# Projecting q and k from a copy of x by columns, with the tokens' mean and scale as rows

## The chip, the cores and the metric

One core of a Trainium2 chip runs the whole kernel. The metric is the device time of one execution in microseconds (us), the median of the runs.

## The reference

```python
x = x + attn(layernorm(x), q_proj, k_proj, v_proj, o_proj)   # x: (1, 2048, 256), 16 heads of 16, causal softmax
x = x + ffn(layernorm(x), W, b, lora_A, lora_B, gate_w, gate_b)
# layernorm: (x - mean) / sqrt(var + 1e-5), over the 256 features
# attn: q, k, v = ln @ W.T; scores / 4; masked softmax; @ v; @ o_proj.T
# ffn: ln @ W.T + b, plus the LoRA updates (8 experts of rank 16) of the two
#      experts with the largest logits, weighted by a softmax over those two
```

All inputs and the output are f32.

## The kernel before

The 2048 tokens are 16 tiles of 128, four tiles a chunk (TPC = 4, CHUNK = 512, NCHUNK = 4). P is 128, KH is 2: the 256 features are two halves of 128 partitions. Every normalised tile is turned on TensorE, because the projections contract over features and so need x with features on partitions, tokens on columns.

The first chunk is projected ahead of everything (`project_first_chunk` on each engine). Then the attention runs in 138 steps. Step s computes two units of scores, 2s and 2s+1 (`scores_of`, L682: f16, two banks a unit, q and k each split in a high and a low f16 part and stacked on 64 rows), takes their exponentials on ScalarE (L814), clears later keys on VectorE one step later (`clear_later_keys`, L999; only units on the diagonal), and multiplies by v into `acc` some steps later (`values_of`, L702, f32). Chunk 0 has steps 0 to 9, chunk 1 steps 10 to 35, chunk 2 steps 36 to 77, chunk 3 steps 78 to 135. On TensorE a step is: the scores of two units, the piece of slot 0, the values of the groups of that step, the piece of slot 1 (only chunk 0 has pieces in slot 1).

Everything else is cut into pieces that share one PSUM bank, `aux`; a piece waits until the piece before it has been read from that bank (`bank_read`, L419). `place_pieces` (L124) gives each piece its step at build time, in order, one a slot. Pieces that prepare the next chunk come first, three for a tile: `turn_x` (L585: two transposes of the normalised tile `xln` by the identity), `project_qk` (L591: 4 blocks x 2 halves, 128 columns each, into all of `aux`), `project_v` (L600). Then `norm_q` and `norm_k`, sums of squares which decide at the end whether the fast softmax was allowed. Then come the pieces after attention, seven for a tile: `turn_sums`, `turn_back`, `o`, `turn_y`, `ffn`, `turn_gated`, `lora`, at most two tiles in work at a time. The four tiles of the last chunk come in a tail behind the steps.

For tile g, VectorE works beside these pieces: `measure_x` (L923: mean and variance), GpSimd the power of -1/2 (`rstd_x`, L1206), VectorE `normalise_x` (L934: `xln`), after the turn `store_xT` (L939), after ScalarE's copy `store_qk` (L801, the f32 result into `qk32`) `split_qk` (L945: high part, low part, clamp, square), and `store_v` (L963). Each engine's program is in a fixed order; VectorE's for a step is in `step` (listing below): normalise_y or the gates of the piece one step before, masks, the work of the piece in slot 0, `keep_sums`, the work of the piece in slot 1.

SyncE issues all DMAs, in a fixed order: the first loads (L431 to L438), q and k of the first chunk out to DRAM and back as stacks (L467 to L475, L450 to L465), the f32 q and k out (L522), `load_rest` (L440), then for each tile `store_parts` (L477: six DMAs), and after the last tile of a chunk 16 loads of stacks. The stack of queries has two buffers, `q_stack[:, c % 2]`; in the opening the second holds `first_parts`.

## Time and profile before

| | us |
|---|---|
| median of 3 runs | 394.41 (393.88 to 394.71) |
| the profiled execution, its own time | 393.18 |
| its span, first to last instruction | 391.4 |
| PE busy | 354.2 (90%) |
| ACT (ScalarE) busy | 279.5 (71%) |
| DVE (VectorE) busy | 209.7 (54%) |
| POOL (GpSimd) busy | 47.8 (12%) |
| mean granted TensorE clock | 0.975 |

The first scores are issued 21.7 us into the span; step 10 begins at 64.1 us; the last values end at 365.3 and the tail ends the span. Busy time of PE counts stretches in which matmuls are in its pipeline; PEld is the loading of weights, which overlaps it. 1.8 us of the profiled execution lie outside its span.

### The profile page before, as it was taken

How to read it: one execution, taken by the hardware profiler on the slowest of the kernel's cores; microseconds unless marked ns; L12 is line 12 of the kernel's file. 1: busy time of each engine (PE TensorE's matmuls, PEld its weight loads, DVE VectorE, ACT ScalarE, POOL GpSimd, SP SyncE). 2: the span in 40 equal slices, each digit the busy share in tenths (PEclk: the TensorE clock that was granted, in tenths of full speed). 3: DMA queues.
4: the chain of work that ended last, by engine and by line, in shares of the span. 5: the costliest groups of instructions: out<-in, count | busy, mean ns of one | idle time of the engine just before them, and what ended most of it. 6: DMA issues, size and time to landing. Idle time of an engine off the chain costs nothing.

```text
span 391.4 us, 6977 instructions
## 1 busy us (share of the span) xinstructions
PE 354.2 (90%) x2558; PEld 138.0 (35%) x2558; DVE 209.7 (54%) x711; ACT 279.5 (71%) x317; POOL 47.8 (12%) x75
## 2 busy tenths in 40 slices
PE   8967978899998999999999999998999899799874
PEld 3545524354333444423323233232322323222542
DVE  4555558455755654555447464546346543600785
ACT  2544438677887877888788887888878688799311
POOL 5011000000011100011121111211112111100040
PEclk9997969999999999999999999999999999999997
DMA  6479444222450022271000000000000000000001
GB/s 202 139 224 315 116 131 141 55 55 54 124 148 13 2 54 75 62 214 44 13 2 13 3 13 16 3 13 2 13 16 0 16 0 15 13 2 3 0 3 55
DMA packets 29380, 23.31 MB, mean 60 GB/s; under 512 B 15392, under 2 KB 25888, under 8 KB 29344
## 3 DMA queue, kind: packets, MB, share of 16 engines
q1 hardware_dynamic: 29344, 22.84, 19.8%
q8 instruction: 21, 0.34, 0.4%
q14 instruction: 15, 0.12, 0.1%
HBM read 12.35 MB, written 10.49 MB: 58 GB/s over the span
## 4 chain that ended last, share of the span: by engine, by line
PE 63%; DVE 20%; ACT 7%; issue 6%; POOL 2%; DMA 1%; DVEq 0%; ACTq 0%
PE acc L713 23%; PE scores L696 12%; PE aux L596 7%; ACT probs L814 6%; PE aux L651 5%; PE aux L637 3%; DVE probs L1010 2%; PE aux L662 2%; PE aux L602 2%; PE aux L623 1%; DVE ffn L1055 1%; POOL exp_gap L1216 1%; PE aux L644 1%; DVE gates L1083 1%; DVE parts L954 1%
## 5 line engine op out<-in xcount | busy, mean ns | idle before, releaser
L814 ACT ACTIVATE probs<-scores 128x1024 f32<-128x1024 f32 x272 | 260.2, 1032 | 69.1 <-PE scores L696 59.1
L713 PE MATMUL acc<-probs,v_aug 128*32 128x512 f32 (+3 forms) x1280 | 145.4, 545 | 1.3 <-ACT probs L814 0.9
L696 PE MATMUL scores<-q_stack,k_stack 64*128 64x512 f16 (+3 forms) x640 | 86.5, 352 | 3.7 <-ACT probs L814 2.0
L696 PEld LDWEIGHTS scores<-q_stack,k_stack 64*128 64x128 f16 x640 | 21.1, 94 | 103.6 <-ACT probs L814 80.3
L1010 DVE TENSOR_TENSOR probs<-probs,mask_sb 128x512 f32<-128x512 f32 (+1 forms) x80 | 44.2, 577 | 22.5 <-ACT probs L814 22.0
L713 PEld LDWEIGHTS acc<-probs,v_aug 128*32 128x32 f32 x1280 | 30.8, 110 | 49.8 <-issue 29.7
L596 PE MATMUL aux<-xT,wqkv_sb 128*128 128x128 f32 x192 | 26.3, 294 | 1.0 <-DVE xT L941 1.0
L596 PEld LDWEIGHTS aux<-xT,wqkv_sb 128*128 128x128 f32 x192 | 24.0, 203 | 5.4 <-issue 3.1
L952 DVE CAST parts<-qk 128x512 f16<-128x512 f32 x12 | 5.1, 427 | 36.5 <-ACT qk L806 36.5
L1207 POOL TENSOR_TENSOR rstd<-ve,minus_half 128x1 f32<-128x1 f32 x12 | 7.3, 608 | 101.6 <-DVE ve L932 101.6
L1211 POOL TENSOR_TENSOR rstd<-ve,minus_half 128x1 f32<-128x1 f32 x12 | 6.6, 549 | 103.8 <-DVE ve L1040 103.8
L651 PE MATMUL aux<-wffn_sb,yT 128*128 128x392 f32 x48 | 19.0, 518 | 0.0
L1033 DVE TENSOR_TENSOR y<-aux,x_sb 128x256 f32<-128x256 f32 x12 | 5.1, 424 | 23.9 <-PE aux L637 23.9
L1216 POOL TENSOR_TENSOR exp_gap<-euler,top_gap 128x1 f32<-128x1 f32 x12 | 6.6, 550 | 86.3 <-DVE top_gap L1068 86.3
L1055 DVE COPY ffn<-aux 128x392 f32<-128x392 f32 x12 | 6.8, 567 | 19.0 <-PE aux L651 19.0
L1015 DVE COPY sums<-acc 128x512 f32<-128x512 f32 x16 | 11.0, 686 | 7.0 <-PE acc L713 7.0
L602 PE MATMUL aux<-wqkv_sb,xT 128*128 128x256 f32 x48 | 13.6, 405 | 1.2 <-ACT qk L806 1.0
L1044 DVE TENSOR_SCALAR yln<-y,mv,rstd 128x256 f32<-128x256 f32 x12 | 9.7, 811 | 8.0 <-POOL rstd L1211 8.0
L637 PE MATMUL aux<-wo_sb,attn_t 128*128 128x256 f32 x48 | 13.6, 405 | 0.0
L1104 DVE TENSOR_TENSOR result<-aux,yb 128x256 f32<-128x256 f32 x12 | 5.1, 425 | 14.7 <-PE aux L662 14.7
L806 ACT COPY qk<-aux 128x512 f32<-128x512 f32 x12 | 7.0, 585 | 8.1 <-PE aux L596 5.6
L657 PE MATMUL aux<-ident_sb,gated 128*128 128x128 f32 x12 | 3.9, 327 | 9.0 <-DVE attn_t L1027 8.1
(146 smaller groups left out, 323.0 us busy)
## 6 DMA issues: line engine op xcount, KB each, us to landing
q_stack<-q_dram SPq DMA_DIRECT2D x32, 128.0 KB, 2.8
k_stack<-k_dram SPq DMA_DIRECT2D x32, 128.0 KB, 2.8
qk_dram<-qk SPq DMA_DIRECT2D x12, 256.0 KB, 2.5
x_sb<-x SPq DMA_DIRECT2D x3, 512.0 KB, 6.4
q_dram<-parts SPq DMA_DIRECT2D x12, 128.0 KB, 2.0
k_dram<-parts SPq DMA_DIRECT2D x48, 32.0 KB, 1.9
out<-result SPq DMA_DIRECT2D x12, 128.0 KB, 1.7
qk_dram<-probs SPq DMA_DIRECT2D x4, 256.0 KB, 3.3
```

The source lines that it names most:

```text
L596: m = pe.matmul(aux[:, n * P:(n + 1) * P], wqkv_sb[:, k, col:col + P], xT[:, k, :], start=(k == 0), stop=(k == KH - 1))
L602: m = pe.matmul(aux[:, 0:D], xT[:, k, :], wqkv_sb[:, k, 2 * D:3 * D], start=(k == 0), stop=(k == KH - 1))
L637: m = pe.matmul(w.bank[:, 0:D], w.attn_t[:, k, :], wo_sb[:, k, :], start=(k == 0), stop=(k == KH - 1))
L651: m = pe.matmul(w.bank[:, 0:FFN], w.yT[:, k, :], wffn_sb[:, k, :], start=(k == 0), stop=(k == KH - 1), skip_group_check=True)
L696: m = pe.matmul(scores[u % BANKS][:, j, col:col + n], k_stack[row:row + STACK, kb // TPC, 2 * i + p, kb % TPC * P:(kb % TPC + 1) * P], q_s ...
L713: m = pe.matmul(acc[32 * hp:32 * hp + 32, lo:CHUNK], v_aug[:, kb, QUAD * i + hp, :], probs[:, u % PROBS, hp % 2, col:col + CHUNK - lo], st ...
L814: act.activation(probs[:, u % PROBS], scores[u % BANKS][:], ACT.Exp, scale=EXP_SCALE).then_inc(exp_done, 1)
L1010: dve.tensor_tensor(tile, tile, mask, ALU.min).then_inc(causal_done, 1)
L1015: dve.tensor_copy(sums[:, c % 3, i, :], acc[:]).then_inc(acc_read, 1)
L1044: dve.tensor_scalar(w.yln, w.y, w.mv2[:, 0:1], w.rstd2, ALU.subtract, ALU.mult).then_inc(yln_ready, 1)
L1055: dve.tensor_copy(w.ffn, w.bank[:, 0:FFN]).then_inc(ffn_ready, 1)
L1216: pool.tensor_tensor(w.exp_gap, euler[:], w.top_gap, ALU.pow).then_inc(gap_exp, 1)
```

## The change

A second input holds x by columns: `x_t`, for each chunk 128 partitions (features) x 2 halves x 512 tokens, 512 KB a chunk, arranged on the host. A chunk is loaded into `xT` by one DMA of SyncE. `xln` and the pieces `turn_x` are gone. VectorE measures the four tiles of a chunk from `x_sb` as before (`measure_x(c, t)`), GpSimd raises all four variances at once, and then stores means and scales (`rows1`, 128 x 2 x 4 values) to DRAM in the order of the tokens, waits for that, waits until the buffer is free, and loads them back as two rows of 512 for every partition, into a part of `q_stack` that isn't in use yet. VectorE then subtracts the row of means from each half of `xT` and multiplies it by the row of scales (`normalise_x(c, k)`, two tensor_tensor of 128 x 512 a half).

`project_qk(n)` now computes one block, q or k of one half of the heads, for all 512 tokens: two matmuls of 512 columns. Four such pieces make a chunk, so their number is the same. `store_qk` and `split_qk` handle such a block; the clamped values go straight into `squares`. SyncE stores a block by one DMA (q) or two (k) and one for the f32 values, 10 a chunk where it was 24, and loads the stacks of a half as soon as its k has landed.

Placing: chunk 0 has its first piece in step 2, then q or k and v in turn, two a step, in steps 2 to 5, and the four norm pieces in steps 6 and 7. For chunk 2 the measurements are at steps 7 to 10, normalise_x at 15 and 16, the four project_qk at 17 to 20, the four project_v at 21 to 24, the norms at 25 and 26. For chunk 3: 33 to 36, 41 and 42, 43 to 46, 47 to 50, 51 and 52. The other pieces keep their order and take the steps left: turn_sums of tile 0 is at step 12 (before: 24), o at 14, turn_sums of tile 1 at 15, turn_y of tile 0 at 16, its ffn at 27; turn_gated of tile 2 is at 53; the last piece is at step 117 (before: 123).

```diff
@@ placing @@
-PRE_PIECES = ("turn_x", "project_qk", "project_v")
+FIRST = ((0, 0), (1, 0), (0, 1), (1, 1))
+FIRST_PIECE = 2
+MEASURE_FROM = {c: FIRST_STEP[c - 1] - 3 for c in range(2, NCHUNK)}
+NORMALISE_FROM = {c: MEASURE_FROM[c] + TPC + 4 for c in range(2, NCHUNK)}
...
-            for g in range(TPC * (c + 1), TPC * (c + 2)):
-                pre += [(name, g) for name in PRE_PIECES]
+            qk = [("project_qk", len(FIRST) * c + n) for n in range(len(FIRST))]
+            v = [("project_v", TPC * (c + 1) + t) for t in range(TPC)]
+            pre = [p for both in zip(qk, v) for p in both] if c == 0 else qk + v
...
-                if pre:
+                if pre and s >= (FIRST_PIECE if c == 0 else NORMALISE_FROM[c + 1] + 2):
@@ tiles @@
-        xln = sb("xln", [P, D])
-        xT = sb("xT", [P, KH, P])
+        rows1 = sb("rows1", [P, 2, TPC])
+        rows = [q_stack[:, b, 0:4].bitcast(F32).rearrange("p (n a) t -> p n (a t)", n=2) for b in range(2)]
+        xT = sb("xT", [P, KH, CHUNK])
@@ sync @@
             sp.dma_start(x_sb[:, TPC:2 * TPC, :], x[:, TPC:2 * TPC, :]).then_inc(x_in[1], 16)
+            sp.dma_start(xT[:], x_t[1]).then_inc(xT_in[1], 16)
+
+            def load_xT(c):
+                sp.wait_ge(v_psum, TPC * (c - 1))
+                sp.dma_start(xT[:], x_t[c]).then_inc(xT_in[c], 16)
...
+            def store_parts(n):
+                c, (kq, m) = n // len(FIRST) + 1, FIRST[n % len(FIRST)]
+                sp.wait_ge(low_ready, n + 1)
+                if kq == 0:
+                    sp.dma_start(q_dram[c, m].rearrange("s p t -> p s t"), parts[:, 0]).then_inc(parts_out[0], 16)
+                else:
                     for s in range(2):
-                        sp.dma_start(k_dram[c, m, :, s, :, tokens], parts[:, b, 1, m, s, :]).then_inc(parts_out[b], 16)
+                        sp.dma_start(k_dram[c, m, :, s], parts[:, 1, s, :]).then_inc(parts_out[1], 16)
+                sp.dma_start(qk32_dram[c, kq, m], qk32[:, kq]).then_inc(qk32_out[kq], 16)
@@ tensor @@
-            def turn_x(g):
-                pe.wait_ge(xln_ready, g - TPC + 1)
+            def project_qk(n):
+                c, (kq, b) = n // len(FIRST) + 1, FIRST[n % len(FIRST)]
+                pe.wait_ge(xT_ready, KH * c)
+                col = column_of(kq, b)
                 for k in range(KH):
-                    t = pe.transpose(aux[:, k * P:(k + 1) * P], xln[:, k * P:(k + 1) * P], ident_sb[:])
-                t.then_inc(xT_psum, 1)
+                    m = pe.matmul(aux[:], wqkv_sb[:, k, col:col + P], xT[:, k, :],
+                                  start=(k == 0), stop=(k == KH - 1))
                 m.then_inc(qk_psum, 1)
@@ vector @@
-                store_first_low(0)
-                store_first_low(1)
-                square_first(0)
-                square_first(1)
-                store_first_low(2)
-                store_first_low(3)
-                square_first(2)
-                square_first(3)
-                measure_x(TPC)
-                normalise_x(TPC)
-                store_xT(TPC)
+                for n in range(len(FIRST)):
+                    store_first_low(n)
+                    measure_x(1, n)
+                for n in range(len(FIRST)):
+                    square_first(n)
...
+            def normalise_x(c, k):
+                n = KH * (c - 1) + k + 1
+                dve.wait_ge(xT_in[c], 16)
+                dve.wait_ge(rows_in, 16 * c)
+                x_rows = xT[:, k, :]
+                dve.tensor_tensor(x_rows, x_rows, rows[c % 2][:, 0, :], ALU.subtract).then_inc(centred, 1)
+                dve.wait_ge(centred, n)
+                dve.tensor_tensor(x_rows, x_rows, rows[c % 2][:, 1, :], ALU.mult).then_inc(xT_ready, 1)
...
+                if s == FIRST_PIECE - 1:
+                    for k in range(KH):
+                        normalise_x(1, k)
+                for c in range(2, NCHUNK):
+                    if 0 <= s - MEASURE_FROM[c] < TPC:
+                        measure_x(c, s - MEASURE_FROM[c])
+                    if 0 <= s - NORMALISE_FROM[c] < KH:
+                        normalise_x(c, s - NORMALISE_FROM[c])
                 for u in (2 * s - 2, 2 * s - 1):
                     if 0 <= u < len(UNITS) and UNITS[u].masked:
                         clear_later_keys(u)
@@ gpsimd @@
-            def rstd_x(g):
-                pool.wait_ge(stats1, STATS1 * (g - TPC + 1))
-                pool.tensor_tensor(rstd1[:], ve1[:], minus_half[:, 0:1], ALU.pow).then_inc(rstd1_ready, 1)
+            def rstd_x(c):
+                pool.wait_ge(stats1, STATS1 * c)
+                if c > 1:
+                    pool.wait_ge(rows_out, 16 * (c - 1))
+                pool.tensor_tensor(rows1[:, 1, :], ve1[:].rearrange("p t o -> p (t o)"), minus_half[:],
+                                   ALU.pow).then_inc(rstd1_ready, 1)
+                pool.wait_ge(means_ready, c)
+                pool.wait_ge(rstd1_ready, c)
+                pool.dma_start(rows_dram[c].rearrange("n (t p) -> p n t", p=P), rows1[:],
+                               allow_slow_non_contiguous=True).then_inc(rows_out, 16)
+                pool.wait_ge(rows_out, 16 * c)
+                if c > 1:
+                    pool.wait_ge(scores_ready, FIRST_UNIT[c - 1])
+                else:
+                    pool.wait_ge(squared, len(FIRST))
+                    for m in range(KH):
+                        pool.wait_ge(first_q_out[m], 16)
+                        pool.wait_ge(first_k_out[m], 16 * 2)
+                pool.dma_start(rows[c % 2], rows_dram[c].partition_broadcast(P)).then_inc(rows_in, 16)
```

## Rows read from the trace of the kernel before

**Rows 1.** Page, parts 1 and 2: busy time; granted TensorE clock in 40 slices (tenths).
```profile
PE 354.2 (90%) x2558; PEld 138.0 (35%) x2558; DVE 209.7 (54%) x711; ACT 279.5 (71%) x317; POOL 47.8 (12%) x75
...
PEclk9997969999999999999999999999999999999997
```

**Rows 2.** Windows: stretch, length, busy of PE, PEld, DVE, ACT, POOL (x), clock, DMA.
```profile
35.50:43.40 7.90, 7.90 (x51) 5.13 (x50) 3.98 (x12) 2.52 (x3) 0.92 (x1) 0.66 0.77 224
...
52.80:64.00 11.20, 10.75 (x99) 4.05 (x98) 7.07 (x13) 6.41 (x7) 0.00 (x0) 0.77 0.68 201
```

**Rows 3.** Chain that ended last, in time: start us, us, engine, tile, line, count.
```profile
10.82 1.72 PE acc L572 x4
...
66.71 1.98 PE aux L596 x16
```

**Rows 4.** Groups by line and shape: total busy us, mean ns, idle before.
```profile
L1010 DVE TENSOR_TENSOR probs<-probs,mask_sb 128x512 f32<-128x512 f32 x48 | 31.9, 684 | 2.8 <-ACT probs L814 2.5
...
L954 DVE TENSOR_TENSOR parts<-qk,parts 128x512 f16<-128x512 f32 x12 | 8.3, 692 | 0.4
...
L588 PE MATMUL aux<-ident_sb,xln 128*128 128x128 f32 x24 | 5.5, 312 | 6.3 <-DVE v_aug L965 5.1 <-DVE xln L936 1.2
...
L806 ACT COPY qk<-aux 128x512 f32<-128x512 f32 x12 | 7.0, 585 | 8.1 <-PE aux L596 5.6 <-DMA qk_dram<-qk 2.5
```

**Rows 5.** DMA issues: queue, count, KB each, median us to landing.
```profile
x_sb<-x SPq DMA_DIRECT2D x3, 512.0 KB, 6.4
q_dram<-parts SPq DMA_DIRECT2D x12, 128.0 KB, 2.0
...
k_dram<-q_stack SPq DMA_DIRECT2D x4, 128.0 KB, 2.4
```

**Rows 6.** Timeline, opening: start us, us, engine line op (idle before, releaser).
```profile
18.21 0.42 DVE L921 TENSOR_TENSOR squares<-squares 128x512 bf16<-128x512 bf16 x1
...
19.55 1.22 SPq L475 DMA_DIRECT2D k_dram<-q_stack  x2
...
24.92 0.43 DVE L952 CAST parts<-qk 128x512 f16<-128x512 f32 x1 [2.70 <-ACT qk L806]
...
26.31 0.43 DVE L959 TENSOR_TENSOR squares<-clamped 128x512 bf16<-128x512 bf16 x1
...
30.49 0.22 PEld L696 LDWEIGHTS scores<-q_stack,k_stack 64*128 64x128 f16 x6
...
60.58 0.61 PE L696 MATMUL scores<-q_stack,k_stack 64*128 64x512 f16 x6
```

**Rows 7.** Timeline of PE: one turn_x piece that waits for VectorE.
```profile
74.54 0.44 PE L588 MATMUL aux<-ident_sb,xln 128*128 128x128 f32 x2 [1.42 <-DVE v_aug L965]
```

**Rows 8.** Timeline, 108 to 114 us: tile 0 after o, tile 1 turned.
```profile
108.81 0.42 DVE L1033 TENSOR_TENSOR y<-aux,x_sb 128x256 f32<-128x256 f32 x1 [1.56 <-PE aux L637]
...
110.83 0.81 DVE L1044 TENSOR_SCALAR yln<-y,mv,rstd 128x256 f32<-128x256 f32 x1 [0.73 <-POOL rstd L1211]
...
112.42 0.97 DVE L1010 TENSOR_TENSOR probs<-probs,mask_sb 128x256 f32<-128x256 f32 x2
...
113.22 0.44 PE L644 MATMUL aux<-ident_sb,yln 128*128 128x128 f32 x2
```

**Rows 9.** Timeline of PE: turn_gated after turn_back, without and with masks beside.
```profile
254.54 0.33 PE L657 MATMUL aux<-ident_sb,gated 128*128 128x128 f32 x1 [0.74 <-DVE attn_t L1027]
...
304.89 0.33 PE L657 MATMUL aux<-ident_sb,gated 128*128 128x128 f32 x1 [1.94 <-DVE attn_t L1027]
```

**Rows 10.** Timeline of PE: scores of four steps with no piece.
```profile
344.88 0.60 PE L696 MATMUL scores<-q_stack,k_stack 64*128 64x512 f16 x4
...
346.41 0.60 PE L696 MATMUL scores<-q_stack,k_stack 64*128 64x512 f16 x4
...
349.54 0.91 PE L696 MATMUL scores<-q_stack,k_stack 64*128 64x512 f16 x4
...
351.37 0.91 PE L696 MATMUL scores<-q_stack,k_stack 64*128 64x512 f16 x4
```

More of the change, by code:

```diff
@@ L317, in transformer_block @@
         stats1 = sem("stats1")
+        means_ready = sem("means_ready")
         rstd1_ready = sem("rstd1_ready")
-        xln_ready = sem("xln_ready")
-        xT_psum = sem("xT_psum")
+        rows_out = sem("rows_out")
+        rows_in = sem("rows_in")
+        xT_in = [sem(f"xT_in{c}") for c in range(NCHUNK)]
+        centred = sem("centred")
         xT_ready = sem("xT_ready")
@@ L663, in lora @@
                           skip_group_check=True).then_inc(out_psum, 1)
-            PRE = {"turn_x": turn_x, "project_qk": project_qk, "project_v": project_v, "norm_q": norm_q,
+            PRE = {"project_qk": project_qk, "project_v": project_v, "norm_q": norm_q,
                    "norm_k": norm_k, "turn_sums": turn_sums}
@@ new lines, in split_qk @@
+            def split_qk(n):
+                c, (kq, m) = n // len(FIRST) + 1, FIRST[n % len(FIRST)]
+                use = n // 2
+                high, low = (parts[:, kq, s, :] for s in range(2))
+                if use:
+                    dve.wait_ge(parts_out[kq], 16 * (kq + 1) * use)
+                dve.wait_ge(qk32_ready, n + 1)
+                dve.tensor_copy(high, qk32[:, kq]).then_inc(high_ready, 1)
+                dve.wait_ge(high_ready, n + 1)
+                dve.tensor_tensor(low, qk32[:, kq], high, ALU.subtract).then_inc(low_ready, 1)
+                block_of = squares[:, c % 2, KH * kq + m, :]
+                if c > 1:
+                    dve.wait_ge(norm_psum, 2 * (c - 2) + kq + 1)
+                dve.tensor_scalar(block_of, high, 1e15, -1e15, ALU.min, ALU.max).then_inc(clamped_ready, 1)
+                dve.wait_ge(clamped_ready, n + 1)
+                dve.tensor_tensor(block_of, block_of, block_of, ALU.mult).then_inc(squared, 1)
@@ L1104, in finish @@
                 dve.tensor_tensor(w.result, w.bank[:, 0:D], w.yb, ALU.add).then_inc(result_ready, 1)
-            PRE = {"turn_x": store_xT, "project_qk": split_qk, "project_v": store_v, "norm_q": norm_q,
+            PRE = {"project_qk": split_qk, "project_v": store_v, "norm_q": norm_q,
                    "norm_k": norm_k}
@@ L1226, in _ @@
                                    minus_half[:, 0:2], ALU.pow).then_inc(first_scale_ready, 1)
-            rstd_x(TPC)
-            rstd_x(TPC + 1)
-            for name, n in PIECES:
-                if name == "turn_x" and n + 1 < TILES:
-                    rstd_x(n + 1)
+            waiting = list(range(2, NCHUNK))
+            rstd_x(1)
+            for s, slot in sorted(PIECE_AT):
+                name, n = PIECE_AT[s, slot]
+                if waiting and s >= MEASURE_FROM[waiting[0]] + TPC:
+                    rstd_x(waiting.pop(0))
                 if name == "o":
```

142 lines of the change are left out of this document (56 added, 86 removed).

## The prediction

> **What bounds the kernel now.** I read the busy times first [rows 1]: PE is busy 354.2 of 391.4 us, so at most 37 us are waits of PE, and the other engines matter by when they release it. Then the windows [rows 2] for where PE is slow rather than idle: at 35.5 to 43.4 us it is busy all the time at a granted clock of 0.66, the first low stretch after it had waited, and 0.77 at 52.8 to 64. Then PE's timeline, step by step. A step with no piece and one group of values takes 1.53 us from scores to scores when PE sets the pace (344.88 to 346.41), and 1.83 us when ScalarE does, with its two exponentials (349.54 to 351.37) [rows 10]. Nearly every step before 123 has a piece, so there PE sets the pace and work taken from it counts in full; a step without a piece gives back only down to 1.83. Last, PE's waits for VectorE inside pieces: 1.42 us at a turn_x [rows 7], 0.74 us at a turn_gated behind the turn_back of the next tile, 1.94 us where two masks stand beside it [rows 9].
>
> **PE's work from chunk 1 on.** Of the 11 turn_x pieces that have a place, 8 lie in steps 10 to 47. The twelve with the one ahead of the steps keep PE busy 5.5 us [rows 4], 0.46 each with an overlap on both sides; I take 0.4, so 8 x 0.4 = 3.2 us. Projecting q and k costs 16 instructions of 128 columns a tile, 1.98 us; the first chunk does the same kind of work with 4 instructions of 512 columns in 1.72 us [rows 3]. Four tiles against four (q or k, half) blocks: 8 x 0.26 = 2.1 us for the two later chunks. project_v is as before. Together -5.3. The waits at turn_x go too: 1.42 [rows 7] and some tenths at another, -1.7.
>
> **What the free steps give back.** With 8 pieces fewer from step 10 on, steps 10 and 11 are empty and the last piece comes at 117 instead of 123. Six more steps at the end run at ScalarE's 1.83 instead of 1.53 plus a piece [rows 10]: 6 x 0.3 = +1.8. Steps 10 and 11 stand beside a heavy one and I give them nothing.
>
> **VectorE's normalising in rows.** It loses 12 copies of xT and 12 xln, and gains 12 tensor_tensor of 128x512 f32, whose nearest rows are the masks, 684 ns, and the low part, 692 ns [rows 4]: 0.69 each, 1.38 us a half. The total barely changes; the place does. VectorE runs its orders in turn, and normalise_x stands ahead of the masks and of the piece of its step. At steps 15 and 16 tile 0 has just left o, and masks are due. The same pieces without it [rows 8]: yln ends at 111.64, the turn of tile 0 comes at 113.22 with no wait. Put 1.38 us and two masks (0.97) behind 111.64, then divide (about 0.75): 114.75. PE has one group instead of two there and would be ready at 112.4: a wait of 2.4. Then at step 16: 1.38, two masks of the wide form (1.3), the yT copy (0.42): 117.9, against a PE that comes to the first project_qk 1.9 after the turn, 116.8: 1.2 more. Together +3.6. Behind the waiting PE stand the scores of the next step, so ScalarE runs dry too. At step 42 the second half stands between the gates of tile 2 and the copy that frees the bank for project_qk: 0.74 [rows 9] becomes 0.74 + 1.38 = 2.1 and it is a wait in a place that had 0.3: +1.8. If cover exists that I don't see (ScalarE behind anyway, the rows read ahead of their step) these two are 0; they can't be more than the 8 x 0.69 = 5.5 us of added work.
>
> **The later pieces in new steps.** turn_gated now meets masks in steps 29, 36 and 67 (1.9 each at most) and none in eight others (0.74) [rows 9]; by the same count three with masks and seven without before, whose waits add up to 9.0 us. Counted out it is +2.2; some of these steps have two groups, which cover it, so +1.5, with 0 and +3 as ends.
>
> **The opening.** Before, VectorE had its first squares done at 18.63 [rows 6]. Now four measurements stand between, which fit the gaps where it waited for ScalarE, but the squares come last. The end of the stats is an estimate: 18.6 less two squares of 0.7 plus 0.9 for one measurement, 18.2; GpSimd's pow, 0.8, gives 19.1. Four squares end near 21.2; the k store of the second half is issued by 20.77 [rows 6] and lands 2.4 us later [rows 5], 23.1. Between lies the store of the rows: 1024 elements of four bytes, from GpSimd, on whose queue the trace shows no DMA. The nearest row is the store of 128 KB in 256-byte runs, 512 of them, 2.0 us to landing [rows 5]; twice as many pieces and another issuer make me take 5, with 2 and 9 as ends: 24.1. Then 512 KB come back, one 4 KB row for each partition: as the loads of x, 6.4 us at worst beside other traffic [rows 5], 5.4 taken: 29.5. normalise_x of both halves is 4 x 0.69 and latencies, 2.9: PE starts the first project_qk at 32.5, in step 2. Scores of steps 0 to 2 are out long before (in the kernel before, step 2 began at 30.49 [rows 6] after one tile of q, k and v). Each of the four rounds is then a ring: q or k 1.72 [rows 3], the copy on ScalarE 0.6 [rows 4], split_qk 1.83 (24.92 to 26.74 [rows 6]), store_v 0.45, latencies 0.4: 5.0. With one keep_sums (0.7) and 0.3 for values that are longer than the cover, 21.0 us: 53.5. The four norm pieces with their reads and four groups take 5.9: step 8 at 59.4 at full clock. Before, step 8 was at 60.58 [rows 6], with two low stretches of the clock in it [rows 2]. PE sits idle from about 26.5 to 32.5 here and is two thirds busy in the ring; a clock between its two levels (2.4 and 1.2 GHz) in the stretch after such a wait is what [rows 2] show, and I charge 2.5 us for it, about what 0.66 over 7.9 us costs. Step 8 at 61.9: +1.3. The ends: with the rows at 2 us the k store decides (23.1), the load takes 4.9, PE starts at 31.0, and with a full clock this is -3; with 9 us and 6.4 it is +6.5. The load of x by columns (512 KB) stands on SP's queue right behind that of x and ahead of the first q store; SP is idle there and the bytes are through about when that store starts, so nothing, 0.6 at most. SP loses 14 of 24 issues a chunk, which ends the 2.5 us for which ScalarE's copy waited for the f32 store [rows 4]; it is in the ring already.
>
> The Trainium skill, DMA: Bandwidth & Descriptors, Rules for kernel authors, says a last dim that isn't contiguous is lowered to one descriptor per element, and gives a DMA from GpSimd about 2 us of fixed cost and 1 us to the first byte (no row here shows either). By an estimate from that page the store of the rows would be near 3 to 4 us plus what 1024 descriptors add, which leaves the forecast where it is.
>
> **Sum.** -5.3 - 1.7 + 1.8 + 3.6 + 1.8 + 1.5 + 1.3 = +3.0, and 0.5 for the two row loads of later chunks: while GpSimd waits for its own store (about 6 us at steps 37 to 39) the rstd of tile 2 stands queued behind it and VectorE's yln, with its masks and copies, behind that. +3.5 on the profiled execution's 393.2 is 396.7; the median of the runs lies 1.2 above that execution, 397.9. I say 397.0.
>
> **Rivals.** (A) Faster: VectorE's added 1.38 us blocks are covered. For it: VectorE is busy only 54% [rows 1] and idle before most of its pieces. Then -5.3 - 1.7 + 1.8 + 1.0, with the opening even: -4, 390. It decides once PE reaches the turn of step 16 no earlier than VectorE, that is once the rows are taken ahead or PE is 2 us later. Against it: VectorE's order is fixed and the masks stand behind. (B) Slower by more: the store of single elements. On GpSimd it isn't 5 but 10 us or more, the first project_qk starts near 38, and every one of the four rounds is behind it: +6 over the sum, 403. It speaks for it that nothing of the kind is in the trace; against, that 512 short runs land in 2.0 us [rows 5]. The Trainium skill, SBUF — State Buffer, The "DVE blocks DMA" trap, adds that GpSimd can't write descriptors while VectorE holds the port they share with a two-port operation; the four squares and the low parts fall into this very time. The rows show only one thing of this sort: yln lasts 0.81 us beside GpSimd's sum [rows 8]. (C) The gain and the costs cancel: within 0.2%, 394.4; where VectorE's waits come to half.
>
> **How the numbers follow.** Forecast 0.45, A 0.30, B 0.17, C 0.08. The range takes the forecast's own ends, A down to 390.5 and most of B: 390.5 to 403.5. A measurement of this kernel tells about 0.2%, 0.8 us, from no change; of the forecast's share nearly all lies above that. Faster 0.31, same 0.09, slower 0.60.
>
> **What would show it.** In the profile after: PE's first project_qk near 32.5 us and its releaser VectorE's xT; the row load landing near 29.5; project_qk as 16 groups of 4 with 1.72 us each; a PE wait near 2 us at turn_y of tile 0 (step 16) and at the first project_qk of each later chunk; no steps at the pace of the exponentials but the last 20. The forecast is wrong if the first project_qk starts before 29, if the waits at steps 16, 17 and 43 come to under 2 us together, or if the clock stays high through the opening.

## The result, and the profile after

The changed kernel takes 430.2 us (median of 4 runs, 429.1 to 430.6) against 394.1 us for the kernel before: a ratio of 1.091, 95% interval 1.088 to 1.094. The forecast was 397.0, its range 390.5 to 403.5. The direction was right, the size was off by 33 us.

The profiled execution has a span of 427.3 us, 35.9 more than before, and a mean granted clock of 0.944. Its page, parts 1, 2 and 4 (the parts of [rows 1] first):

```profile
PE 354.9 (83%) x2390; PEld 121.6 (28%) x2390; DVE 207.2 (49%) x693; ACT 279.6 (65%) x317; POOL 49.2 (12%) x72
...
PEclk9965999988999988889999999999999999999996
...
PE 48%; DVE 22%; DMA 10%; issue 8%; ACT 6%; POOL 3%; SPq 1%; DVEq 0%; ACTq 0%; POOLq 0%
```

PE is busy as long as before (354.2), so the 36 us are waits, though it has 168 instructions fewer: what was saved went into stretches of low clock, in slices 3 and 4, 9 and 10, 15 to 18 (before: slices 4 and 6). A tenth of the chain that ended last is DMA.

Read by steps (start of step 10, of step 53, of step 135, in us): before 64.1, 174.5, 360.5; after 74.3, 209.2, 395.3. So the opening lost 10.2, steps 10 to 53 lost 24.5, steps 53 to 135 lost 0.1 and the tail 1.2. The two windows of after (columns as in [rows 2]; before, 64.1 to 174.5 had PE 105.3 of 110.4 us busy at a clock of 1.00):

```profile
74.30:209.20 134.90, 114.60 (x754) 37.71 (x750) 67.44 (x192) 88.04 (x96) 13.45 (x18) 0.92 0.25 77
209.20:395.30 186.10, 171.84 (x1265) 51.08 (x1266) 81.51 (x296) 155.31 (x164) 22.44 (x36) 1.00 0.03 8
```

PE's longest waits in all of after (engine, tile, line, the one who ended them: us, times, longest). L655 is turn_y, L605 project_qk, L668 turn_gated:

```profile
PE aux L605 <- DVE xT L953: 15.7, 1, 15.7
PE aux L655 <- DVE attn_y L1031: 15.3, 8, 5.7
PE aux L668 <- DVE attn_t L1036: 10.9, 10, 2.2
...
PE aux L605 <- DVE attn_t L1036: 2.1, 1, 2.1
```

Before, the waits at turn_y came to 0.6 us from step 10 on and those at turn_gated to 8.1. The opening, by the timelines of GpSimd, VectorE and PE (they answer to [rows 6]): the store of the rows, the load of the rows, the first half normalised, the first project_qk:

```profile
19.84 1.09 POOL L1230 DMA_DIRECT2D rows_dram<-rows  x1 [0.61 <-POOL rows L1226]
31.56 0.58 POOL L1240 DMA_DIRECT2D q_stack<-rows_dram  x1 [10.64 <-DMA k_dram<-q_stack]
...
38.59 0.69 DVE L951 TENSOR_TENSOR xT<-xT,q_stack 128x512 f32<-128x512 f32 x1 [17.77 <-DMA q_stack<-rows_dram]
...
41.48 3.60 PE L605 MATMUL aux<-xT,wqkv_sb 128*128 128x512 f32 x4 [15.72 <-DVE xT L953]
```

GpSimd waits 10.6 us, and the releaser named is the store of k of the second half. It is two DMAs, one issued 0.3 us ahead of the rows' issue and one 0.3 us after that began; they land after 6.6 and 10.8 us, against the 2.4 of [rows 5]. Loads suffer too: the four of the queries, issued at 22.3 to 24.2 us, land after 9.1 to 9.3 us, where the median of their kind is 2.9. In the windows of that stretch (last columns: clock, DMA share, GB/s) the DMA engines are more than half busy from 25 to 31 us and move 48 and 37 GB/s; the third window, with the load of the rows in it, moves 271:

```profile
25.00:28.00 3.00, 0.61 (x2) 0.10 (x2) 0.00 (x0) 2.85 (x4) 0.00 (x0) 0.50 0.69 48
28.00:31.00 3.00, 0.00 (x0) 0.00 (x0) 0.00 (x0) 0.00 (x0) 0.00 (x0) 0.50 0.56 37
31.00:38.60 7.60, 0.00 (x0) 0.00 (x0) 0.01 (x1) 0.00 (x0) 0.58 (x1) 0.50 0.86 271
```

The same store comes back for chunks 2 and 3 (GpSimd, then what stood behind it):

```profile
78.01 0.94 POOL L1230 DMA_DIRECT2D rows_dram<-rows  x1 [0.56 <-POOL rows L1226]
86.79 0.56 POOL L1240 DMA_DIRECT2D q_stack<-rows_dram  x1 [7.83 <-DMA rows_dram<-rows]
...
91.62 0.69 DVE L951 TENSOR_TENSOR xT<-xT,q_stack 128x512 f32<-128x512 f32 x1 [2.82 <-DMA q_stack<-rows_dram]
...
94.39 0.69 PE L655 MATMUL aux<-ident_sb,yln 128*128 128x128 f32 x2 [5.21 <-DVE attn_y L1031]
...
166.46 0.57 POOL L1240 DMA_DIRECT2D q_stack<-rows_dram  x1 [10.00 <-DMA rows_dram<-rows]
...
169.13 0.69 PE L655 MATMUL aux<-ident_sb,yln 128*128 128x128 f32 x2 [5.71 <-DVE attn_y L1031]
```

The first of them holds VectorE through normalise_x; the second holds GpSimd, behind which stood the rstd of tile 2.

### The profile page after: what moved, and what is told of

Read it like the earlier page. It is cut to its first block, busy times and chain, and to the rows that moved or that the text cites. A ratio compares the mean times of both kernels' runs of the same rounds, so it can differ in the third digit from the quotient of the medians.

```text
span 427.3 us, 6598 instructions
## 1 busy us (share of the span) xinstructions
PE 354.9 (83%) x2390; PEld 121.6 (28%) x2390; DVE 207.2 (49%) x693; ACT 279.6 (65%) x317; POOL 49.2 (12%) x72
## 4 chain that ended last, share of the span: by engine, by line
PE 48%; DVE 22%; DMA 10%; issue 8%; ACT 6%; POOL 3%; SPq 1%; DVEq 0%; ACTq 0%; POOLq 0%
PE acc L727 17%; PE scores L710 8%; PE aux L605 6%; ACT probs L828 5%; DMA rows_dram<-rows 4%; PE aux L662 4%; DMA q_stack<-rows_dram 3%; DMA k_dram<-q_stack 3%; PE aux L648 3%; DVE probs L1019 2%; PE aux L613 2%; PE aux L673 2%; DVE ffn L1064 1%; DVE gates L1092 1%; POOL exp_gap L1249 1%
## 5 line engine op out<-in xcount | busy, mean ns | idle before, releaser
L710 PE MATMUL scores<-q_stack,k_stack 64*128 64x512 f16 (+3 forms) x640 | 87.9, 355 | 8.3 <-ACT probs L828 4.6
L605 PE MATMUL aux<-xT,wqkv_sb 128*128 128x512 f32 x48 | 27.3, 696 | 19.6 <-DVE xT L953 15.7
L662 PE MATMUL aux<-wffn_sb,yT 128*128 128x392 f32 x48 | 19.9, 540 | 0.0
L1244 POOL TENSOR_TENSOR rstd<-ve,minus_half 128x1 f32<-128x1 f32 x12 | 6.6, 553 | 113.4 <-DVE ve L1049 113.3
L655 PE MATMUL aux<-ident_sb,yln 128*128 128x128 f32 x24 | 5.8, 325 | 15.3 <-DVE attn_y L1031 15.3
L605 PEld LDWEIGHTS aux<-xT,wqkv_sb 128*128 128x128 f32 x48 | 9.1, 211 | 31.7 <-issue 24.5
L951 DVE TENSOR_TENSOR xT<-xT,q_stack 128x512 f32<-128x512 f32 x6 | 4.1, 688 | 21.0 <-DMA q_stack<-rows_dram 21.0
L668 PE MATMUL aux<-ident_sb,gated 128*128 128x128 f32 x12 | 3.9, 326 | 11.8 <-DVE attn_t L1036 10.9
```

The source lines that it names most:

```text
L605: m = pe.matmul(aux[:], wqkv_sb[:, k, col:col + P], xT[:, k, :], start=(k == 0), stop=(k == KH - 1))
L662: m = pe.matmul(w.bank[:, 0:FFN], w.yT[:, k, :], wffn_sb[:, k, :], start=(k == 0), stop=(k == KH - 1), skip_group_check=True)
L710: m = pe.matmul(scores[u % BANKS][:, j, col:col + n], k_stack[row:row + STACK, kb // TPC, 2 * i + p, kb % TPC * P:(kb % TPC + 1) * P], q_s ...
```

## The experiments

Ratios are to the kernel before, run on the same chip beside each kernel. Theory S says that the store of single elements is the loss, rival Q that it is GpSimd's queue. Later runs ask for the rest.

**The element store as 256 runs.** Tokens get one another's mean and scale here, since the rows are stored in another order than they are read; bytes and instructions are the same.

```diff
-pool.dma_start(rows_dram[c].rearrange("n (t p) -> p n t", p=P), rows1[:], ...)
+pool.dma_start(rows_dram[c].rearrange("n (p t) -> p n t", p=P), rows1[:], ...)
```

> Means and scales are stored as 256 runs of 16 bytes (each partition's four together) instead of 1024 single elements of four bytes, so that the tokens get one another's means and scales; issuer, bytes, waits and everything else are the changed kernel's. Theory S (the single elements are what makes the store last 9 to 11 us, and what holds other stores back in the opening): the store lands in about 3 us, the k store issued at 19.6 us lands in 2.4 instead of 10.8, the first project_qk starts near 32 instead of 41.5, the wait of 5.7 us at turn_y of tile 2 goes, and the time is 397 to 404. Rival Q (the queue of GpSimd is slow whatever it carries): store still 9 to 11 us, time 428 to 431.

411.0 us, ratio 1.042 (1.035 to 1.049): 19 us less, by swapping two letters. GpSimd's two issues, PE's first project_qk, and PE at turn_y of step 16:

```profile
21.42 0.90 POOL L1230 DMA_DIRECT2D rows_dram<-rows  x1 [0.61 <-POOL rows L1226]
26.35 0.59 POOL L1240 DMA_DIRECT2D q_stack<-rows_dram  x1 [4.04 <-DMA k_dram<-q_stack]
...
34.27 3.75 PE L605 MATMUL aux<-xT,wqkv_sb 128*128 128x512 f32 x4 [6.89 <-DVE xT L953]
...
84.05 0.44 PE L655 MATMUL aux<-ident_sb,yln 128*128 128x128 f32 x2 [1.93 <-DVE attn_y L1031]
```

Step 10 starts at 67.3 instead of 74.3, and steps 10 to 53 take 122.5 us instead of 134.9: the store cost 7.0 us in the opening and 12.4 in the two later chunks (7.7 of these are PE's idle time, the rest its work at a lower clock). The 7.0 is rather low: this execution had a stretch of low clock ahead of its first scores, which come at 23.4 us and not at 21.8 as in after; from there to step 10 the difference is 8.7. In the opening the rows land after 4.2 us, not 3, the two stores of k after 4.2 and 4.0, not 2.4, and the first project_qk is 2 us later than theory S had it. And 411.0 isn't its 397 to 404: something else costs 12.1 us in steps 10 to 53 (before: 110.4).

**Count or neighbourhood?** The kernel above with a second store of 1024 single elements, 256 bytes from one to the next, for which GpSimd waits too.

> As the kernel with runs of 16 bytes, plus a second store of the 1024 single elements, each 256 bytes from the next in DRAM, and GpSimd waits for both. If the number of elements is what costs, this store takes 9 to 11 us again and the time is 425 to 435. If it is that neighbouring elements fall into the same few bytes of DRAM one after the other, the spread store takes some 3 to 4 us and the time is 398 to 406.

412.2 us (1.040 to 1.051). The three spaced stores land after 3.7, 3.9 and 5.5 us, the longest in the opening, where GpSimd waits 5.1:

```profile
22.35 0.92 POOL L1234 DMA_DIRECT2D rows_wide<-rows  x1
28.37 0.58 POOL L1245 DMA_DIRECT2D q_stack<-rows_dram  x1 [5.11 <-DMA rows_wide<-rows]
```

So as many elements, spread out, don't take 9 to 11 us. They aren't free either: in the profiled executions GpSimd's load is issued 2.0 us later than with runs alone and step 10 starts at 71.2 instead of 67.3. The time is above the 398 to 406 of the expectation for the same reason as before: the loss that isn't the store's.

**The issuer.** The element store as in the changed kernel, issued by ScalarE.

> The changed kernel with the store of single elements issued by ScalarE instead of GpSimd, same elements, same places; the load stays with GpSimd. Theory S: the store still takes 9 to 11 us, opening and later waits stay, time 426 to 434. Rival Q (GpSimd's queue): store near 3 us, time 397 to 405.

428.6 us (1.081 to 1.092), and PE's first project_qk at 40.39 instead of 41.48. Q is out: who issues it doesn't matter.

**The store by itself.** Two kernels append single DMAs to the kernel before, each waited for; their whole time says nothing.

```diff
+def apart(w):    # 1024 elements, 4 * w bytes from one to the next; partition p writes elements p, p + 128, ...
+    return dest[w].rearrange("(j p) w -> p j w", p=P)[:, :, 0:1]
+pool.dma_start(to, few[:].unsqueeze(2), allow_slow_non_contiguous=True).then_inc(priced, 16)
+pool.wait_ge(priced, 16 * count)
```

> The kernel before with stores of four-byte elements one after another behind its end, all from GpSimd, nothing else running: 1024 elements next to each other in DRAM (in the order of the change, so that neighbours come from different partitions), the same with 16, 32, 64, 128 and 256 bytes from one to the next, 512 elements next to each other, 256 runs of 16 bytes, 128 runs of 32 bytes; the whole twice. Then a store of 128 KB from SP alone, with the dense 1024 elements issued by GpSimd beside it, and with the 256-byte spaced ones. Theory L (elements that share a few bytes of DRAM hold each other up): dense 8 to 11 us, falling to 3 to 4 by 64 bytes or before, 512 dense near half of it; the 128 KB store 2.4 alone and beside the spaced ones, 7 or more beside the dense ones. Rival C (the load of the rest of the opening made it slow): dense and spaced within 1 us of each other here, and the 128 KB store the same in all three.

In the timeline of GpSimd, the bracket of each line is the wait for the DMA of the line above: 4, 16, 32 bytes apart, then (further down) 512 dense elements, 256 runs of 16 bytes and 128 runs of 32:

```profile
391.65 1.05 POOL L1275 DMA_DIRECT2D dest<-few  x1 [0.40 <-POOL few L1263]
401.76 0.89 POOL L1275 DMA_DIRECT2D dest<-few  x1 [9.06 <-DMA dest<-few]
405.58 0.89 POOL L1275 DMA_DIRECT2D dest<-few  x1 [2.92 <-DMA dest<-few]
408.90 0.88 POOL L1275 DMA_DIRECT2D dest<-few  x1 [2.44 <-DMA dest<-few]
...
419.03 0.76 POOL L1275 DMA_DIRECT2D half<-few  x1 [2.43 <-DMA dest<-few]
428.27 0.71 POOL L1275 DMA_DIRECT2D runs<-few  x1 [8.48 <-DMA half<-few]
431.20 0.58 POOL L1275 DMA_DIRECT2D runs<-few  x1 [2.22 <-DMA runs<-few]
433.19 0.90 POOL L1275 DMA_DIRECT2D dest<-few  x1 [1.41 <-DMA runs<-few]
```

From issue to the next issue: 10.1 us dense, 3.8 at 16 bytes, 3.3 at 32, and 3.3 to 3.4 at 64, 128 and 256; 2.9 for the runs of 16. Half as many dense elements take 9.2 us. Over both kernels the dense store takes 9.0 to 10.1, half of it 8.4 to 9.3. Theory L holds for the distance and fails for the number. The 128 KB store landed after 1.7 us both alone and beside the dense elements; but it had moved its bytes before they began.

> The kernel before with more stores of four-byte elements behind its end, all from GpSimd and each alone: 1024 elements 4, 8, 12 and 16 bytes from one to the next, then 128, 256 and 512 of them next to each other (one, two and four for each partition); the whole twice. Then a store of 128 KB from SP: alone, and issued just after the dense 1024 elements and just after the same number 256 bytes apart. Theory L (writes that fall into the same few bytes wait for each other): the time goes down with the distance, 8 bytes near 5 to 6 us, and does not go down with the number, since each stretch of DRAM still gets as many; 128 dense elements 7 us or more. Rival N (what counts is how many unmerged elements there are): 128 dense near 2.5 us, 8 bytes near 10. For the 128 KB store: if engines are held by the dense elements it lands after 7 us or more beside them; if only lines of DRAM are, after 3 us or less.

8 bytes apart takes 4.2 to 4.3 us, 12 bytes 4.6 to 4.9. The wait after 128 dense elements (one from each partition, second line), and the waits for the 128 KB store alone (3.04) and issued behind the dense elements (10.88):

```profile
412.76 0.56 POOL L1275 DMA_DIRECT2D half<-few  x1 [2.85 <-DMA dest<-few]
420.85 0.71 POOL L1275 DMA_DIRECT2D half<-few  x1 [7.53 <-DMA half<-few]
...
487.52 0.89 POOL L1290 DMA_DIRECT2D dest<-few  x1 [3.04 <-DMA plain<-x_sb]
488.40 0.12 POOL L1292 MEMSET marks<- 128x1 f32 x1
499.40 0.88 POOL L1290 DMA_DIRECT2D dest<-few  x1 [10.88 <-DMA plain<-x_sb]
```

The three plain stores, from issue to landing, and the DMA engines (busy tenths in 40 slices) from 488 to 499 us, with what was issued in it:

```profile
DMA to landing us min/median/max: 2.4/2.7/10.3
...
DMA  0001907600000000000000000000000000000000
...
plain<-x_sb SPq DMA_DIRECT2D x1, 128.0 KB, 10.3
dest<-few POOLq DMA_DIRECT2D x1, 4.0 KB, 10.6
```

128 dense elements take 8.1 us (7.1 the second time), nearly as long as 1024. And the 128 KB store of SP's own queue lands after 2.7 us alone, 2.4 behind spaced elements and 10.3 behind dense ones. Its packets aren't late: those of both DMAs are over by 490.2 us, and then the engines are empty until both land, at 498.1 and 498.9. What the dense elements hold back here is the landing, their own and that of a store whose packets came behind theirs. The store of k in the changed kernel lands late beside the same elements. There loads wait as well and the engines are more than half busy, which the single stores don't show. The Trainium skill, DMA: Bandwidth & Descriptors, Specifications, says that a transfer below 512 bytes is done by read-modify-write. That would fit writes that wait for their neighbours; but at 32 bytes apart nothing of it is left here, so the unit that they share is not 512 bytes. Why neighbours wait isn't shown by these runs, nor whether it matters that they come from different partitions. The same page, Rules for kernel authors, says that such a store is lowered to one descriptor per element; with one element in every 256 bytes that costs 3.3 us here, and the dense store takes three times as long.

**Rows without DRAM.** TensorE makes the rows: `rows1[:, n, t]`, broadcast along its free axis, as weights against the identity, four matmuls into one bank; VectorE reads them from PSUM. The first piece is in step 0 again; in chunks 2 and 3 the rows are two pieces more, 1.1 us each.

> No round trip through DRAM: TensorE multiplies each column of means and scales, repeated over 128 columns, by the identity, so that PSUM holds the row on all partitions; VectorE subtracts and multiplies from PSUM. Chunk 1 has it before step 0, so the first project_qk may stand in step 0; chunks 2 and 3 have two pieces more each. If the round trip carries all of the loss of the opening and the waits for GpSimd, the first project_qk starts near 24 us, step 10 near 58 (before: 64.1), and the sum of the rest (PE's work -5 plus 2 for the four new pieces, VectorE's waits +5, free steps +2) makes 389 to 393. If wide projection or the load of x by columns costs more than I think, it stays above 396.

402.4 us, ratio 1.022 (1.017 to 1.026): not the 389 to 393 but the other expectation, above 396. Step 10 starts at 63.5, so the opening is even with before; steps 10 to 135 lose 9.7 us. The trace names two things. One is in the opening: ScalarE's copy of the third block waits for SP's f32 store, which SP issues behind the loads of x and of the later weights:

```profile
40.81 0.58 ACT L830 COPY qk<-aux 128x512 f32<-128x512 f32 x1 [6.29 <-DMA qk_dram<-qk]
```

The other is what the wide projection is worth, a term of the sum. At full clock, here a line of after; in this kernel it is the same:

```profile
102.06 1.98 PE L605 MATMUL aux<-xT,wqkv_sb 128*128 128x512 f32 x4
```

Start to start with what follows it is 1.91 us, against 1.98 for the 16 narrow ones of [rows 3]: 0.07 a piece.

**The places.** The kernel above, with the rows of chunks 2 and 3 at steps 10 and 36 and the projections right behind, and every piece after attention in exactly the step of the kernel before.

```diff
-MEASURE_FROM = {c: FIRST_STEP[c - 1] - 3 for c in range(2, NCHUNK)}
-NORMALISE_FROM = {c: MEASURE_FROM[c] + TPC + 4 for c in range(2, NCHUNK)}
+MEASURE_FROM = {c: FIRST_STEP[c - 1] - 5 for c in range(2, NCHUNK)}
+NORMALISE_FROM = {c: FIRST_STEP[c - 1] for c in range(2, NCHUNK)}
+                if 0 < c < NCHUNK - 1 and s < FIRST_STEP[c] + 3 * TPC + 2:
+                    continue
```

> The kernel with the rows made by TensorE (402.4 us) still loses 9 to 10 us against the kernel before between steps 10 and 135, though its opening is even. Here its pieces of chunks 2 and 3 begin at steps 10 and 36 (measured five steps earlier) and the pieces after attention stand in exactly the steps of the kernel before, up to step 123. Theory P, the places (pieces that meet masks and each other's VectorE work): that loss goes. By rows of the profiles: four rows pieces of 1.1 (+4.4), eight turn_x of 0.4 gone (-3.2), eight q and k projections at 1.91 instead of 1.98 (-0.6), turn_x waits gone (-1.7), opening -0.6: 392.5, with a wait or two in the new pieces 393 to 396. Theory W, the work itself (VectorE's wide operations ahead of masks, lower clock): 400 to 404, and PE's waits at turn_gated stay near 13 us in all instead of 9.

395.7 us, ratio 1.006 (1.004 to 1.008): 6.7 us less for the same instructions (6.2 by the two ratios; the kernel before was 1.3 us faster beside this one). PE's waits at turn_gated are 8.1 us again, as in the kernel before. Theory P.

The same question the other way round: the kernel before, with nothing changed but that its pieces ahead of attention may start only in steps 17 and 43.

```diff
-                if pre:
+                if pre and s >= {0: 0, 1: 17, 2: 43}.get(c, 0):
```

> The kernel before with one edit: the pieces of chunks 2 and 3 ahead of attention (turn_x, project_qk, project_v, norms) may start only from steps 17 and 43, as in the changed kernel, so that pieces after attention stand in steps 12 to 16 and 31 to 42 as there. Everything else is as before: nothing by columns, no rows. Theory P: where the pieces stand costs time by itself, 4 to 8 us (e5_place against the kernel with rows from TensorE was 6.7): 398 to 402, with PE's waits at turn_gated and turn_y near 13 us instead of 9. Rival N: places cost only beside the change's wide VectorE work: within 2 us of the kernel before.

404.3 us, ratio 1.027 (1.023 to 1.030): 10.6 us, more than I gave it. By the steps of the profiled execution 2.5 come in steps 10 to 53 and 10.2 in 53 to 135; its opening, the same code as before, was 2.4 shorter and had one stretch of low clock instead of two. PE waits over 0.9 us ten times in steps 11 to 134 instead of five, and some of these waits are followed by a low clock. A wait, and the 5 us behind each of two such waits; the last line is the kernel before behind the longest of its own, 1.94 us [rows 9]:

```profile
213.84 0.33 PE L657 MATMUL aux<-ident_sb,gated 128*128 128x128 f32 x1 [1.94 <-DVE attn_t L1027]
```

```profile
122.10:127.10 5.00, 5.00 (x29) 1.35 (x33) 0.72 (x2) 1.83 (x2) 0.00 (x0) 0.66 0.58 179
...
213.80:218.80 5.00, 4.96 (x35) 1.51 (x35) 1.49 (x4) 1.94 (x2) 0.00 (x0) 0.66 0.02 3
```

```profile
304.80:309.80 5.00, 4.91 (x43) 2.21 (x47) 1.66 (x5) 2.78 (x4) 0.00 (x0) 1.00 0.09 30
```

Over 5 us a clock of 0.66 costs 1.7 us, nearly as much as the wait itself. Waits of the same length are followed by 0.66 in one place and 1.00 in another; what decides which isn't settled by these runs.

**SP's order.** First the loads moved behind chunk 1's stores, in step 4.

> As e5_place, and the loads of x of chunks 2 and 3 and of the weights after attention are issued in step 4, behind the stores and stack loads of chunk 1, instead of ahead of them. In the kernel with the rows from TensorE, ScalarE's copy of the third wide block waited 6.3 us for the f32 store that SP issues behind those loads, and PE's project_v behind the copy. Theory: SP's queue sets that wait; step 10 comes 4 to 6 us earlier and the time is 3 to 6 us under e5_place. Rival: the queue of copies and of VectorE's splits would be late anyway, or the loads now stand in the way of the stacks of chunk 1: within 1 us of e5_place.

396.2 us (1.004 to 1.011), no gain: ScalarE's wait went, and VectorE came to measure chunk 2 before its x had arrived; PE waited 9.1 us at the norm piece behind it. So the loads were split:

```diff
+                if s == 3:
+                    sp.dma_start(x_sb[:, 2 * TPC:3 * TPC, :], x[:, 2 * TPC:3 * TPC, :]).then_inc(x_in[2], 16)
+                if s == 6:
+                    load_rest()
```

> e5_place with the loads after chunk 1's opening split: x of chunk 2 is issued in step 3, x of chunk 3 and the weights after attention in step 6, and chunk 2 is measured in steps 6 to 9. In e6_sp ScalarE's copy no longer waited, but VectorE came to measure chunk 2 in step 5 before its x had been loaded and PE waited 9.1 us at the norm piece behind it, so nothing was tried of the gain itself. Theory: both waits go, ScalarE's 6.4 us and VectorE's, and with them the low clock behind them; step 10 comes 3 to 6 us before e5_place's 63.6, the time is 389.5 to 392.5, under the kernel before by 0.3% or more. Rival: a further wait in the ring of q, k and v stands right behind: step 10 within 1 us of 63.6 and 395 to 396.

387.9 us, ratio 0.985 (0.981 to 0.989): faster than both kernels, and below the 389.5 of the theory. Step 10 starts at 56.9, and in the profiled execution the clock no longer drops in the opening:

```profile
PE 352.0 (91%) x2438; PEld 125.6 (32%) x2438; DVE 208.2 (54%) x693; ACT 280.1 (72%) x317; POOL 43.9 (11%) x66
...
PEclk9999999999999999999999999999999899899996
```

**Two and four steps earlier.** The same kernel without the two empty steps of chunk 1 and the two of chunk 2, so that the pieces after attention stand two steps earlier up to step 35 and four from there on.

> e9_split (387.9 us) without its two empty steps: the pieces after attention start in steps 22 and 48, so all later ones stand two steps earlier against the masks and groups of values. The work is the same to the instruction. Theory P, what counts is which step each turn meets: PE's waits at turn_gated and turn_y from step 27 on change from 8 to 9 us in all to 12 or more, each followed by a stretch of lower clock, and the time is 391 to 396. Rival: what cost 6.7 and 10.6 us was only the pieces put ahead of the projections in steps 12 to 16 and 36 to 42: the two steps saved give nothing or a little, 387 to 388.5.

393.6 us, ratio 0.998 (0.995 to 1.001): theory P again, 5.6 us (5.2 by the ratios) for a shift of two to four steps and not one instruction more. PE waits 1.76, 1.61 and 1.67 us at steps 29, 33 and 36; behind the first two the clock is 0.66 for 5 us. But the kernel with the empty steps has two such low stretches as well, behind its waits at steps 108 and 122, which are shorter or gone here. In the profiled executions, 3.7 us apart, it is PE's idle time that makes the difference: 3.4 us more in steps 10 to 135. At turn_gated and turn_y it came to 11.6 us against 9.8, less than the 12 or more of the expectation.

**A control.** How much of the 1.5% is SP's order alone? The kernel before, with its loads split.

> The kernel before with the loads after its opening split as in e9_split: x of chunk 2 is issued in step 2, x of chunk 3 and the weights after attention in step 6. A control: how much of e9_split's 1.5% is the order of loads and how much the columns. In the kernel before ScalarE's copy waited 2.5 us in all for the f32 store [rows 4]. Theory K (columns and wide pieces are worth something once the rest is cured): 391 to 394, e9_split stays 3 us or more under it. Rival O (the order of the loads is all there is): 387 to 390.

401.5 us (1.016 to 1.023), but by a wait of its own: PE and VectorE wait in step 10 for the weights after attention, which SP issues at 63.9 us here.

```profile
PE scores L699 <- DMA expert_ids_sb<-expert_ids: 7.6, 1, 7.6
```

> e12_before_split with PE's and VectorE's wait for the weights after attention moved from step 10 to step 24, just ahead of their first use. The wait of 7.6 us at step 10 goes; what is left is the kernel before with SP's loads in the order of e9_split. Theory K (the columns and wide pieces are worth something once the rest is cured): 391 to 394, e9_split stays 3 us or more under it. Rival O (the order of the loads is all there is): 387 to 390.

391.4 us, ratio 0.992 (0.989 to 0.995). Half of the gain is the order of the loads. The other half, 3.4 us between the medians and 2.8 by the ratios, would belong to the columns and what came with them; the two intervals just touch. Where it comes from isn't shown. In the profiled executions step 10 starts at 56.9 against 64.6, but that of the control was its longest (395.2), and from its first scores to step 10 the clock was 0.80 against 1.00. A fifth of those 43.0 us is 8.6, enough for the whole 7.7:

```profile
PEclk9968889999999999999999999999999899999995
```

From step 10 to 135 the two take 299.3 and 298.0 us, so that there the rows pieces (4.4) cost at least what the turns and wide projections save. With the loads in the old order the columns bring nothing: that is the 395.7 us above.

**Rows through DRAM, in runs, and early.** The two rows pieces of chunks 2 and 3 against the DMA of 16-byte runs, VectorE reading the rows with a stride.

> As e6_sp for the opening (rows of chunk 1 made by TensorE) and for the places after attention; the rows of chunks 2 and 3 go through DRAM, in 256 runs of 16 bytes and read back by VectorE with a stride, early enough: measured from steps 3 and 26, normalised in steps 9, 10 and 34, 35. x of chunk 2 is loaded in step 2. Theory: the four rows pieces of 1.1 us on PE were paid in full, so 3 to 5 us under e6_sp, and PE never waits more than 1 us for xT. Rival: with the rows through DRAM VectorE's or GpSimd's waits for the store and load (2.6 and up to 7 us) come back on PE: as e6_sp or above it.

405.0 us, ratio 1.030 (1.024 to 1.035), 9 us worse than with TensorE. The rows of chunk 2 come in at 68.7; read with a stride, each of the four operations takes 1.09 us instead of 0.69, masks stand between and behind, and PE waits:

```profile
68.78 1.09 DVE L970 TENSOR_TENSOR xT<-xT,squares 128x512 f32<-128x512 f32 x1 [3.89 <-DMA squares<-rows_dram]
...
74.73 3.75 PE L620 MATMUL aux<-xT,wqkv_sb 128*128 128x512 f32 x4 [5.38 <-DVE xT L972]
```

Step 17 starts 6.6 us behind the kernel with TensorE's rows and all loads in step 4, with step 10 even. A wait of 5.4 us and half a clock behind it cost more than four pieces of 1.1.

## Why the prediction was right in direction and wrong in size

The sum was +3.5 us; the trace has +35.9. The direction doesn't hang on the store: with the rows stored in runs the kernel is still 4% slower than before. Two steps failed: the price of the store of the rows, with who waits for it in the later chunks, and what new places cost the later pieces.

**PE's work, -5.3.** Turn_x was sized right: the stages that lost their eight pieces lost 3.1 us, for 3.2 put down. The wide projection was mis-sized: 1.91 us instead of 1.72, so 8 x 0.07 = 0.6 and not 2.1. The 1.72 of [rows 3] is a projection that follows its like; one that stands between other pieces doesn't have it. The waits at turn_x (-1.7) did go.

**The opening, +1.3; measured +10.2.** The failing step is "twice as many pieces and another issuer make me take 5, with 2 and 9 as ends". GpSimd's wait for it and for the store of k was over 11.1 us after its issue, at about 31: outside the ends, because it was bounded by a store of short runs, and because the store of k was taken as landing at 23.1 on its own; it landed at 31.0. The load took 6.9 instead of 5.4, and the 6.4 that was taken for the worst of its kind is a median. All else held: the two normalise_x 2.9 us, for 2.9; from the first project_qk to step 8 29.3 us, for 29.4. Rival B had the mechanism, "10 us or more", and its first project_qk near 38; it was 41.5.

**The row loads of later chunks, +0.5.** This is the largest miss: 12.4 us (after against the kernel with runs, steps 10 to 53). The line of reasoning was written down, GpSimd behind its own store and the rstd of tile 2 behind it, yet with a store of 6 us and no price for who waits. Rival B carried its 10 us into the opening alone; worked through, its 403 would have been 415.

**VectorE's normalising, +3.6 and +1.8.** Right where it can be seen without the store: at turn_y of step 16 PE waits 1.93 us in the kernel with runs (2.4 forecast), at the first project_qk of step 43 2.06, in after as well (2.1 forecast). At step 17 it waits 0.89 in the kernel with runs (1.2 forecast); in after nothing, behind the 5.2 us of step 16.

**The later pieces in new steps, +1.5, ends 0 and +3.** Mis-sized by a factor of about four or more: 6.7 us (to the places of before), 5.6 (a shift of two to four steps), 10.6 (the kernel before with late pieces). The count took only turn_gated and only the wait. For turn_gated it held: its waits are 11.8 us in after against 9.0, so +2.8, though the +2.2 can't be had from the numbers beside it (3 x 1.9 and 8 x 0.74 are 11.6, 2.6 over the 9.0). What was left out, without a reason, are the waits at turn_y and the low clock. Turn_y has 4.4 us in the kernel with runs, that of step 16 apart, against 0.6 before. In the kernel with late pieces the waits at turn_gated rose by 4.1 us, those at turn_y by 3.9, and PE's busy time for the same work by 4.8, its clock granted at 0.98 instead of 1.00.

**What the free steps give back, +1.8.** Steps 53 to 135 took 186.1 us against 186.0, with some 4.3 us of pieces fewer in them. PE's idle time there rose by 3.7 us: 2.7 at turn_y, 0.2 at turn_gated and 0.8 behind ScalarE (scores 1.7 more, values 0.9 less). So the pieces saved came back as waits; what of it is the free steps, put down at 1.8, can't be told apart.

**What would show it.** The first project_qk was to be near 32.5 with xT as its releaser: the releaser was right, the time 9 late. "The load landing near 29.5": 38.5. The clock was low in the opening, as charged, but at 0.50 from 25 us to the first project_qk and not between the levels. None of the three signs of a wrong forecast came, since all three look to the fast side; a first project_qk behind 37.5, where the 9 us and the 6.4 lead, would have been the one to name. The sum of the known causes: store 19.4 (7.0 and 12.4), the rest of the opening 3.2, steps 10 to 53 12.1, the end 1.2, together 35.9. Of the 12.1, 4.3 are pieces done earlier (by their durations), -3.7 what PE saved, and 11.5 waits and the clock behind them. Of these 7.6 are idle time of PE: 4.9 where normalise_x stands ahead (steps 16, 17 and 43), 2.6 more at turn_gated, 1.1 more at turn_y, 1.7 less at turn_x, and small ones. The rest is its work at a clock of 0.97 instead of 1.00. No run tries the normalising and the places apart; with TensorE's rows the move back to the old places was worth 6.7.

## What to carry to other kernels

Give each partition a run of its own in DRAM before anything else is tuned: single four-byte elements whose neighbours come from other partitions took 7 to 10 us here, 128 of them nearly as long as 1024, and the landings of other queues' stores waited with them. In a pipeline with an order fixed by hand, a change that moves pieces is two changes: measure it with the old places kept, since two to four steps to the side were worth 5.6 us here, more than the work that was saved. When a wait is charged, allow for a low clock behind it too: in the kernel with late pieces it followed the three waits of 1.8 to 1.9 us and cost 1.7 us each time, while in the kernel before it didn't follow one of 1.94. And follow a slow DMA to every place where it is issued, not only the first.

## What the runs showed of the hardware that I had not expected

- 1024 stored elements of 4 bytes: 9.0 to 10.1 us dense, 4.2 to 4.3 with 8 bytes from one to the next, 3.6 to 4.0 at 16, 3.3 to 3.5 from 32 bytes on; 128 dense 7.1 to 8.1. With ScalarE as issuer the changed kernel takes 428.6 us instead of 430.2.
- A plain store of 128 KB from another queue: 2.7 us alone, 2.4 behind spaced elements, 10.3 behind dense ones, with its packets over 1.6 us after its issue.
- Four f32 matmuls of 512 columns as a piece between others take 1.91 us start to start, sixteen of 128 columns 1.98: 0.07 us for wide operands.
- VectorE reading one f32 operand 16 bytes from one element to the next, beside a dense one: 1.09 us for 128x512, 0.69 when both are dense.
